# Mixture-of-experts tail of a transformer block: scatter-adds of one expert side by side, routing split 14 + 2, slot turns later

## The reference, cut to what matters

```python
x = x + xcond(layernorm(x), ctx, ctx, itok)     # 8 batches x 256 rows of 512; "channel" attention
x = x + ffn(layernorm(x), ...)
# ffn: T = 2048 tokens, D = 512, E = 8 experts, K = 2, cap = 320, hidden 2048, rank 32
probs = softmax(xt @ gate_w); top_p, top_i = top_k(probs, 2)
for k in range(2):
    e, w = top_i[:, k], top_p[:, k]
    pos = running count of e over the tokens; keep = pos < cap
    buf[e, pos] = xt                             # per expert at most cap rows
    h = gelu(buf @ w1 + b1); y = h @ w2 + b2 + gelu(buf @ wd) @ wu
    out += keep * w * y[e, pos]
out = out + 0.2 * (gelu(xt @ sw1 + sb1) @ sw2 + sb2 + gelu(xt @ swd) @ swu)
```

## Time and profile before

| what | us |
|---|---|
| median of 3 runs | 1555.46 (1554.65 to 1556.03) |
| the profiled execution | 1552.73 |
| its span, first to last instruction | 1550.9 |
| PE busy in the span | 1425.4 (92%) |
| DVE, ACT, POOL busy | 779.4, 697.4, 234.2 |

### The profile page before, as it was taken

How to read it: one execution, slowest core, us unless ns; L and a number is a source line. 1 busy time by engine, 2 the same in 40 slices (tenths; PEclk the granted TensorE clock), 3 DMA queues, 4 the chain that set the end, 5 groups by cost and what they waited for, 6 DMA issues and landing times. The chain is left out here.

```text
span 1550.9 us, 27116 instructions
## 1 busy us (share of the span) xinstructions
PE 1425.4 (92%) x11352; PEld 1000.7 (65%) x11368; DVE 779.4 (50%) x1287; ACT 697.4 (45%) x1015; POOL 234.2 (15%) x219
## 2 busy tenths in 40 slices
PE   2569999999999999988799999999999999999992
PEld 1126372726364544536488889998888888888882
DVE  5477565756565747644462543626345262453600
ACT  3446455464646373733443434435344443434401
POOL 6240000000000001052300301212020120210102
PEclk8689999999999999999799999999999999999997
DMA  8410213122222222011732544436343352542202
GB/s 259 157 45 24 75 48 89 49 82 55 76 62 69 69 69 51 6 29 38 247 119 84 142 125 127 123 101 154 111 134 105 121 143 84 142 122 79 46 1 34
DMA packets 92058, 143.30 MB, mean 92 GB/s; under 512 B 15401, under 2 KB 36025, under 8 KB 91938
## 3 DMA queue, kind: packets, MB, share of 16 engines
q1 hardware_dynamic: 79218, 115.98, 23.0%
q0 software_dynamic: 12288, 25.21, 9.2%
q10 hardware_dynamic: 432, 0.39, 0.1%
HBM read 109.47 MB, written 32.06 MB: 91 GB/s over the span
## 5 line engine op out<-in xcount | busy, mean ns | idle before, releaser
L1530 PE MATMUL banks<-hidden,w2h 128*128 128x0 bf16 x2048 | 324.5, 275 | 0.0
L1530 PEld LDWEIGHTS banks<-hidden,w2h 128*128 128x128 bf16 x2048 | 198.2, 98 | 29.3
L828 ACT ACTIVATE hidden<-banks,scales 128x512 f32<-128x512 f32 x256 | 163.6, 685 | 108.9 <-PE banks L1350 101.2
L1530 PE MATMUL banks<-hidden,w2l 128*128 128x0 bf16 x1024 | 198.5, 275 | 0.0
L1023 DVE TENSOR_REDUCE rowmax<-banks 128x1 f32<-128x512 f32 x256 | 170.5, 680 | 46.7 <-PE banks L1320 45.9
L917 ACT ACTIVATE hf<-banks,b1cols 128x640 f32<-128x640 f32 x128 | 101.7, 794 | 181.9 <-PE banks L1505 179.2
L1430 PE MATMUL banks<-w2h,hidden 128*128 128x512 bf16 x512 | 181.3, 383 | 0.0
L1149 DVE TENSOR_TENSOR w1l<-stage,w1h 128x2048 bf16<-128x2048 f32 x32 | 73.3, 2292 | 200.0 <-ACT w1h L893 200.0
L1320 PE MATMUL banks<-KS,QS 96*128 96x512 bf16 x256 | 100.7, 402 | 38.8 <-DVE rowmax L1023 27.2
L1505 PE MATMUL banks<-eth,w1l 128*128 128x0 bf16 x1024 | 135.9, 276 | 0.0
L1505 PE MATMUL banks<-eth,w1h 128*128 128x0 bf16 x1024 | 135.9, 276 | 0.0
(11 more groups left out here) (174 smaller groups left out, 2021.5 us busy)
## 6 DMA issues: line engine op xcount, KB each, us to landing
stage<-in_L_ffn_w SPq DMA_DIRECT2D x64, 1024.0 KB, 5.3
split_parts<-hidden SPq DMA_DIRECT2D x16, 512.0 KB, 3.1
QS<-split_parts SPq DMA_DIRECT2D x48, 128.0 KB, 2.5
KS<-split_parts SPq DMA_DIRECT2D x45, 128.0 KB, 2.8
xin<-in_x SPq DMA_DIRECT2D x16, 256.0 KB, 2.7
cin<-in_ctx SPq DMA_DIRECT2D x16, 256.0 KB, 2.9
out_rows<-xin SPq DMA_DIRECT2D x16, 256.0 KB, 2.0
normed_rows<-x2r SPq DMA_DIRECT2D x16, 256.0 KB, 2.0
```

Source lines behind the costliest of these rows:

```text
L828: ac.activation(prob[n % NPH], bank(score_bank[unit]), ACT.Exp, scale=scales[:, g // 2:g // 2 + 1]).then_inc(s_exp, 1)
L1530: issued = mm(half_of(bank(b0 + j)).shape_from_register(bank_cols(e, j)), w[:, fb, rows], half_of(a[:, fb, :], j).shape_from_register(slot ...
```

## The change

Four things are changed.

1. Adds of one expert no longer wait for one another: POOL waits for all earlier adds only at c = 0. For that, empty slots get rows of their own for each chunk: row T + 128c + partition. `out_rows` and `normed_rows` grow from 2048 + 128 to 2048 + 640 rows, and SP fills ten blocks of 128 rows with zeros at `start_routing` where it filled two.
2. The five chunks of expert 7 are written not to the three `yout` buffers but to five pieces of `stage`, which hold no weights any more then; ACT waits once for the last split instead of for adds, and the adds count on a semaphore of their own.
3. EARLY_GROUPS is 14: part 0 of the routing covers 14 groups and 28 scatters, part 1 two groups and 4 scatters. Part 1 is spread over the steps of `shared_up(7)` as 4 operations at each of the first five steps, then 2, none, and 6 at a step.
4. The turns of expert 0 begin after 23 steps of `shared_down(7, ...)` and not after 14.

```diff
-EARLY_GROUPS = GROUPS - 4
+EARLY_GROUPS = GROUPS - 2
+
+ROWS = T + SLOTS
...
-    for _ in shared_up(7):
-        one_of(routing, 3)
+    for n, _ in enumerate(shared_up(7)):
+        one_of(routing, 4 if n < 5 else 2 if n == 5 else 0 if n == 6 else 6)
...
-        if i >= 13:
+        if i >= 22:
             next(turning, None)
...
+        last_rows = [stage[c // 4][:, c % 4 * D:c % 4 * D + D] for c in range(CH)]
...
-                    dma(xn_rows[T:T + P, :], zrows[:, :]).then_inc(s_fill, 16)
-                    dma(out[T:T + P, :], zrows[:, :].bitcast(F32)).then_inc(s_fill, 16)
+                    for c in range(CH):
+                        rows = slice(T + c * P, T + c * P + P)
+                        dma(xn_rows[rows, :], zrows[:, :]).then_inc(s_fill, 16)
+                        dma(out[rows, :], zrows[:, :].bitcast(F32)).then_inc(s_fill, 16)
...
-                    gp.iota(empty[:, :, 0], pattern=[[0, E * CH]], base=T, channel_multiplier=1).then_inc(s_iota, 1)
+                    gp.iota(empty[:, :, 0].rearrange("p (e c) -> p e c", c=CH), pattern=[[0, E], [P, CH]], base=T,
+                            channel_multiplier=1).then_inc(s_iota, 1)
...
+                    if c == 0:
+
+                        for r in range(3):
+                            pool.wait_ge(s_yst[r], yst_before(n, r))
                     pool.wait_ge(s_y, n + 1)
-                    for r in range(3):
-                        pool.wait_ge(s_yst[r], yst_before(n, r))
+                    rows, landed = (yout[n % 3], s_yst[n % 3]) if e < E - 1 else (last_rows[c], s_last)
                     gp.indirect_dma_start(out=out, out_offset=bass.IndirectOffsetOnAxis(ap=slots[:, e, c, 0:1], axis=0),
-                                          in_=yout[n % 3][:, :], in_offset=None, bounds_check=T + P - 1, oob_is_err=True,
-                                          compute_op=ALU.add).then_inc(s_yst[n % 3], 16)
+                                          in_=rows[:, :], in_offset=None, bounds_check=ROWS - 1, oob_is_err=True,
+                                          compute_op=ALU.add).then_inc(landed, 16)
...
-                    act.wait_ge(s_yst[n % 3], 16 * (n // 3))
+                    if e < E - 1:
+                        act.wait_ge(s_yst[n % 3], 16 * (n // 3))
+                    elif c == 0:
+                        act.wait_ge(s_wlo, 8 * E)
```

More of the change, by code:

```diff
@@ L365, in build @@
         parts_dram = nc.dram_tensor("split_parts", [2, 4, P, L], BF16, kind="Internal").ap()
-        xn_rows = nc.dram_tensor("normed_rows", [T + P, 2 * D], BF16, kind="Internal").ap()
+        xn_rows = nc.dram_tensor("normed_rows", [ROWS, 2 * D], BF16, kind="Internal").ap()
         table = nc.dram_tensor("slot_table", [E * SLOTS, 2], I32, kind="Internal").ap()
@@ L505, in build @@
         s_yst = [sem(f"s_yst{i}") for i in range(3)]
+        s_last = sem("s_last")
         s_hstage = [sem(f"s_hstage{i}") for i in range(8)]
@@ L677, in sync_program @@
                         dma(stage[n % NST][:, :].rearrange("p (a w) -> p a w", w=512), src).then_inc(s_stage[n % NST], 16)
-            n = GROUPS + E * CH
+            n = GROUPS + (E - 1) * CH
             for r in range(3):
@@ L684, in sync_program @@
                 sp.wait_ge(s_x2st[r], 16 * (GROUPS // 2))
-            sp.wait_ge(s_fill, 48)
+            sp.wait_ge(s_fill, 16 * (1 + 2 * CH))
+            sp.wait_ge(s_last, 16 * CH)
             sp.wait_ge(s_scatter, 16 * GROUPS * TOPK)
@@ L757, in pool_program @@
                         pool.wait_ge(s_iota, 7)
-                        pool.wait_ge(s_fill, 48)
+                        pool.wait_ge(s_fill, 16 * (1 + 2 * CH))
                         pool.wait_ge(s_entry, 1 if g == 0 else 2)
@@ L777, in pool_program @@
                                               in_offset=bass.IndirectOffsetOnAxis(ap=slots[:, e, c, 0:1], axis=0),
-                                              bounds_check=T + P - 1, oob_is_err=True).then_inc(s_gather, 16)
+                                              bounds_check=ROWS - 1, oob_is_err=True).then_inc(s_gather, 16)
                 elif kind == "e_y":
@@ L928, in act_program @@
                     act.wait_ge(s_yt, e * CH + c + 1)
-                    act.wait_ge(s_yst[n % 3], 16 * (n // 3))
+                    if e < E - 1:
+                        act.wait_ge(s_yst[n % 3], 16 * (n // 3))
+                    elif c == 0:
+                        act.wait_ge(s_wlo, 8 * E)
                     if e == 0 and c == 0:
                         act.wait_ge(s_table, 16)
-                    ac.activation(yout[n % 3][:, :], bank(4 + (e * CH + c) % 2), ACT.Copy,
+                    ac.activation(yout[n % 3][:, :] if e < E - 1 else last_rows[c][:, :], bank(4 + (e * CH + c) % 2), ACT.Copy,
                                   scale=slots[:, e, c, 1:2].bitcast(F32)).then_inc(s_y, 1)
@@ L1584 @@
         args.append(nc.dram_tensor(f"in_{name}", a.shape, mybir.dt.from_np(a.dtype), kind="ExternalInput").ap())
-    out = nc.dram_tensor("out_rows", (T + P, D), F32, kind="ExternalOutput").ap()
+    out = nc.dram_tensor("out_rows", (ROWS, D), F32, kind="ExternalOutput").ap()
     build(nc, *args, out)
```

## The result

| kernel | median us | runs |
|---|---|---|
| before | 1555.74 (1554.65 to 1558.88) | 4 |
| changed | 1527.16 (1526.00 to 1534.02) | 4 |
| ratio | 0.9823, 95% interval 0.9804 to 0.9842 | |

The changed kernel's profiled execution took 1527.68 us, its span is 1525.9 (before: 1550.9); for the profiled execution 1524.2 had been forecast. Both places behave as forecast in kind. First the end: timeline of POOL in the changed kernel, the five adds of expert 7, the rows that answer to the earlier trace rows (start, us, engine, line, output<-input, idle before).

The account below looks back on a forecast made before the run. PE, busy 92% of the span, was taken as the bound. Gains of 15.0 at the end and 14.2 at the passage, less 0.7, made 28.5: 1555.46 - 28.5 = 1527.0 us, range 1521 to 1537.

Parts of the forecast that it names:

- The end: Expert 7's five final adds: issued 1.85 us apart instead of 5.60, end 6.24 after the last issue; gain 15.0.
- just the pace of issue, so no line builds up: Expert 7's adds: each takes 1.9 us of all sixteen DMA engines, against an issue step of 1.85.
- The passage: Routing part 1 to expert 0: entry 3.1 us earlier, gathers 8.4 earlier, expert 0 at 750.3, not 764.54; gain 14.2.
- Gathers and PE arrive together: Before expert 0's first turn: gathers landed near 739, PE there at 738.6; 0.4 of the 14.62 us wait left.
- What is late next: Before expert 0: ACT's in-order weight casts and copies leave PE idle some 2.7 us in two or three pieces.
- up to 2 more: Bound on the passage: PE's new idle of 2.7 us may cost clock, up to 2 us more.
- A clock of 0.5 after 748: Sign of being wrong at the passage: PE at half clock after 748, where full clock through 740 to 755 was forecast.
- (a): At the end, adds slow one another or their issue, 3.98 a step; gain there 6.5, time 1535.5; chance 0.12.
- (b): At the end, POOL can hold only one add in flight; 5.60 a step stay, time 1542.0; chance 0.05.
- (c): Passage gains 9 to 11 only, through late weight load or half clock after the gap; about 1531; chance 0.13.
- (d): PE's 3.82 gap at 667 ends as POOL's twelve scatters end; avoided 1521.3, a second one 1533; chance 0.08.
- (e): Slower than before: ACT waits for buffers of adds in flight, each taking 18.8 us; over 1558.6; chance 0.02.

Follow-up runs that it names:

- e9: The kernel before, unchanged, traced on the same chip as the changed kernel; 1542.67 us, ratio 0.9997.
- e10: The changed kernel, unchanged, traced on one chip beside the kernel before; 1519.69 us, ratio 0.9847.
- e1: The changed kernel with the passage as before, so only the changes to the adds remain; 1536.67 us, ratio 0.9898.
- e3: The changed kernel once more, no edit, on another chip's set of runs; 1522.54 us, ratio 0.9802.
- e12: The changed kernel with expert 7's five final adds moving only the first 256 of 512 columns per row; 1519.7 us, ratio 0.9848.
- e2: The kernel before with only the passage changed: routing split 14 + 2, new spread, turns after 23 steps; 1539.8 us, ratio 0.9928.
- e4: The changed kernel with expert 0's third and fourth weight casts moved behind the copies of the turned slots; 1524.74 us, ratio 0.9816.
- e8: The changed kernel with expert 0's five turns two down steps apart, from step 23 on; 1517.46 us, ratio 0.9832.
- e11: The changed kernel with the five turns two down steps apart, run again beside the unedited changed kernel; 1517.39 us, ratio 0.9824.
- e7: The changed kernel without its 32 scatters into the slot table, so the experts add nothing; 1515.89 us, ratio 0.9818.
- the first group: Follow-up runs e1, e2, e3 and e4, on one chip beside the kernel before, whose median there was 1552.82 us.
- the other two groups: The second and third groups of follow-up runs, each on one chip; the kernel before had medians of 1542.91 and 1543.41 us.

## Why the prediction came out right, point by point

**The end.** The mechanism and the pace are right (1.865 for 1.85). The term is 15.0, measured 13.9 in the first pair and 14.1 between e9 and e10. The step that failed is "just the pace of issue, so no line builds up". I had multiplied the share of a window of 6.00 us (0.34) by a step of 5.60 and got 1.9 us of all sixteen engines per add. A window of exactly one step of the kernel before gives more:

```profile
1527.83:1533.52 5.69, 0.00 (x0) 0.00 (x0) 0.00 (x0) 0.69 (x1) 1.58 (x2) 0.52 0.35 46
```

That is 2.0 for an add alone, and five in flight need 2.0 each as well (the DMA view of the changed kernel: their queue takes 67.6% of sixteen engines over the 15 us from 1511 to 1526, that is 10.1, a fifth each). So it was not the flight side by side that made adds dearer: 2.0 was above the pace of 1.865 from the start, and by estimate four steps leave a line of 4 x (2.0 - 1.865), about 0.5. Measured it is more. The end follows the last issue by 6.24 to 6.38 in the five traces with adds one by one, and by 6.99 to 7.91 in the eight with whole rows side by side: 0.7 to 1.1 in the two pairs compared, up to 1.7 in e1 and e3. What makes it differ among equal adds stays open. e12 fits: there an add takes 1.18 of sixteen engines (share 0.47 over 7.46 us and 0.45 over 5.27, a fifth), below the pace, so no line; by estimate 6.24 less the 0.8 that the add is shorter gives 5.4, against 5.27. The 6.24 behind the last add was a time for one add alone and should not have been carried over.

The Trainium skill, "DMA: Bandwidth & Descriptors", section "Anatomy of one DMA — SWDGE (gpsimd) path", gives 2.0 us plus bytes at 436 GB/s for such a DMA, by estimate 2.6 here. The median landing of the five adds of expert 7 is 5.2 in the changed kernel's trace and 4.7 in that of the kernel before, each alone there, so the trace does not agree (the landing times of the earlier trace rows are those of all DMAs that touch `out_rows`; its forty adds alone have 4.6, 4.8 and 9.1); and in its windows the engines are full at 120 GB/s.

**The passage.** Each of its steps can be read off the table of e9 and e10: entry 3.4 earlier for 3.1, the gathers 9.1 for 8.4, `e_rank` 15.1 for 14.2. The wait before the first turn, forecast 0.4, is 0 in the changed kernel's traces with fast gathers (the first one and e10; also e2 and e4) and 2.3 to 3.1 in e3, e8, e11 and e12. "Gathers and PE arrive together" was true, and so a spread of 3 us in the gathers, which before had no meaning beside 14.62, now decides about a wait. What is late next was right in kind: ACT's copies, 2.14 at `e_rank` where I had 2.7. The chain of casts and copies that I added up is what ACT did in e10, without a gap. What I had not seen is that the last turns' place sets the same moment by itself (e4), so that moving the casts gains nothing.

**The costs.** `place` came 0.65 to 0.68 later (0.7). The wait of group 15's `norm2` behind one scatter more is 0.43 on PE in e10 where I had 0.2 at most; e7 shows that it is the scatters' doing. Why it is twice the 0.2 is not shown.

**The clock.** The half-clock stretch behind the 14.62 is gone with it in e10. The bound of "up to 2 more" for the new wait was needed: a stop of 2.1 to 2.2 before `e_rank` brought half clock in the first trace of the changed kernel, in e4, e7 and e12, 1.7 us each (first up step 4.94 after `e_rank` instead of 3.27), and none in e2, e3, e5 and e10. The granted clock is 0.63 over 752.00 to 756.60 in the first trace and 1.00 over 744 to 748 in e10. Nothing in the rows tells why one and not the other. "A clock of 0.5 after 748" stood among the signs of being wrong, and the first trace of the changed kernel had it, and a stop of 2.18 at another place; so by its own signs the passage was only partly right there.

**The rivals.** (a) and (b) fall by the five rows of POOL. (c), a passage of 9 to 11 only, is what e3's trace has (10.2), through the 3.02 for the gathers and not through late weights. (d) looked at a real thing from the wrong side. The stop near 667 is in all six traces of the first pair and the first group, 2.3 to 3.8 long, whatever the order, and in none of the eight traces of the other two groups. A row of ACT's timeline in the kernel before (first pair), and then a window of e9, columns as above:

```profile
670.43 1.27 ACT L828 ACTIVATE hidden<-banks,scales 128x512 f32<-128x512 f32 x2 [5.17 <-remote]
```

```profile
660.00:680.00 20.00, 20.00 (x124) 6.17 (x121) 11.60 (x18) 9.06 (x15) 15.66 (x17) 1.00 0.09 28
```

In before ACT stands still too, until 670.43, and PE goes on at 671.17; POOL goes on issuing its scatters meanwhile, 1.29 apart. In e9 PE is busy for 20.00 of 20.00 at a clock of 1.00, with the same twelve scatters in front. So neither the order nor the scatters by themselves make the stop; the chip or the execution does. Its cause stays open: e7 was made to show it and ran where there was nothing to show. (e) never came near: in the traces of the changed kernel no engine waits for an add to `out_rows`.

**What was luck.** The forecast 1527.0 against 1527.16 is closer than the working deserves. In the first pair the profiled executions differ by 25.0: 3.3 of start-up, 4.6 of PE's stops (98.75 - 93.08 less the 1.08 of e10) and 1.7 of half clock moved the sum, partly against each other. In the three sets of runs that have both kernels the medians gave 28.6, 30.3 and 23.7 us, and the profiled execution of the first pair took 1527.68 where 1524.2 was forecast. The 28.1 of e9 and e10, piece by piece, is what bears out the working.

## What to carry to other kernels

Where transfers are taken off each other's completion, ask for three paces: of the issue (0.30 + 1.55 here), of the producer, and of the DMA engines with all of them in flight. The slowest sets the time; here the engines' 2.0 against an issue pace of 1.865 made the tail of the last add 0.7 to 1.7 longer. Where a wait is removed by letting two chains arrive together, the spread of the later one, harmless before, becomes the next wait. Starting the consumer one step later did not cover it here (e8 and e11 still waited 2.3 and 2.8); more steps were not tried. And put the last consumers so that something covers what follows them: two steps apart, the wait for the copies was 1.18 instead of 2.1 to 2.2. And compare pieces between marks that stand in both programs, on one chip, before believing a sum.

## What was not expected of the hardware

Indirect adds of 128 rows of 2 KB fill all sixteen DMA engines (share 1.00 to 1.01) at 120 to 131 GB/s, where weights and gathers move 392 at 1.05; half the bytes per row brought the share to 0.59. The same program's gathers came in two manners, the fifth issue 1.01 or 2.3 to 3.1 long. Stops of PE of 2.1 to 2.2 before `e_rank` brought half clock in some executions and not in others. And the kernel before lay at medians of 1555.74 and 1552.82 in two sets of runs and at 1542.91 and 1543.41 in the two others. Between its two traces (spans 1550.9 and 1540.3) PE's stop near 667 with its half clock, T12 to T15 93.08 against 86.61, is 6.5 of the 10.6, and the start-up 3.8.
